# Loading the first six adjacency quarters of a graph-attention kernel as halves

## The reference, cut to what matters

```python
def _L0_gnn_ref(input1, input2, adj, a1, a2):      # N = M = 4096, D = 128
    e = input1 @ a1 + (input2 @ a2).T
    e = jnp.where(e > 0, e, 0.2 * e)
    att = jnp.where(adj > 0, e, NEG)
    att = jax.nn.softmax(att, axis=1)
    deg = jnp.sum(adj, axis=1, keepdims=True)
    att = att * deg
    att = GAMMA * att + (1.0 - GAMMA) * adj
    return att @ input2

x = x + _L0_gnn_ref(_layernorm(x, axis=-1), L0_gnn_input2, adj, L0_gnn_a1, L0_gnn_a2)
x = x + _L0_ffn_ref(_layernorm(x, axis=-1)[None], L0_ffn_weight, L0_ffn_bias)[0]
```

## Time and profile before

| | us |
|---|---|
| median of 3 runs (377.69 to 378.69) | 378.52 |
| the profiled execution: its time | 376.63 |
| the profiled execution: its span | 374.8 |
| PE busy in that span | 357.4 (95%) |
| DVE busy | 311.4 (83%) |
| ACT busy | 252.9 (67%) |
| POOL busy | 146.6 (39%) |
| the 16 DMA engines: POOL's queue, share of their span | 47.0% |

### The profile page before, as it was taken

How to read it: one execution, slowest core, us unless ns; L and a number is a source line. 1 busy time by engine, 2 the same in 40 slices (tenths; PEclk the granted TensorE clock), 3 DMA queues, 4 the chain that set the end, 5 groups by cost and what they waited for, 6 DMA issues and landing times.

```text
span 374.8 us, 8950 instructions
## 1 busy us (share of the span) xinstructions
PE 357.4 (95%) x3199; PEld 313.6 (84%) x3199; DVE 311.4 (83%) x787; ACT 252.9 (67%) x616; POOL 146.6 (39%) x258
## 2 busy tenths in 40 slices
PE   5689999999999799999999999999999999999992
PEld 5578888888888688888888888888888888888881
DVE  5998989969999768879788888989687887999832
ACT  5799896697588568392947749294874929897100
POOL 4594713805262532608043260806225160703111
PEclk9999999999999999999999999999999999999998
DMA  7999959492959596694929487591958830121000
GB/s 251 202 214 202 218 110 183 78 192 45 171 119 174 117 144 136 81 202 89 204 45 181 91 145 139 96 199 42 160 118 117 160 72 2 32 26 44 30 18 30
DMA packets 34646, 45.72 MB, mean 122 GB/s; under 512 B 18084, under 2 KB 25896, under 8 KB 34600
## 3 DMA queue, kind: packets, MB, share of 16 engines
q0 software_dynamic: 9216, 33.56, 47.0%
q1 hardware_dynamic: 25384, 11.56, 16.4%
HBM read 74.84 MB, written 3.82 MB: 210 GB/s over the span
## 4 chain that ended last, share of the span: by engine, by line
PE 77%; DMA 8%; issue 5%; DVE 3%; POOL 2%; ACT 2%; SPq 1%; POOLq 0%; DVEq 0%
PE acc_u L760 23%; PE acc_v L763 23%; PE acc_y L742 21%; PE acc_v L742 4%; DMA adj_all<-adj 4%; PE acc_u L742 3%; DMA late<-block_rows 3%; PE acc_y L731 2%; PE small L725 2%; ACT steep L554 2%; DMA s_rows<-pre_s 1%; DVE plus L972 1%; POOL adj_all L409 1%; SPq L330 1%; PE acc_u L731 0%
## 5 line engine op out<-in xcount | busy, mean ns | idle before, releaser
L554 ACT ACTIVATE steep<-s_bc,steep_s 128x256 bf16<-128x256 f32 x512 | 218.2, 524 | 13.1 <-DMA s_bc<-s_rows 6.6
L763 PE MATMUL acc_v<-weights_v,minus 128*128 128x258 f16 x896 | 198.1, 272 | 0.0
L760 PE MATMUL acc_u<-weights_u,plus 128*128 128x258 f16 x896 | 198.1, 273 | 0.0
L742 PE MATMUL acc_y<-weights_y,adj_all 128*128 128x257 f16 x896 | 101.3, 273 | 0.4 <-DMA adj_all<-adj 0.4
L742 PEld LDWEIGHTS acc_y<-weights_y,adj_all 128*128 128x128 bf16 x896 | 86.8, 97 | 12.5 <-DMA adj_all<-adj 0.7
L760 PEld LDWEIGHTS acc_u<-weights_u,plus 128*128 128x128 bf16 x896 | 86.7, 97 | 12.0
L763 PEld LDWEIGHTS acc_v<-weights_v,minus 128*128 128x128 bf16 x896 | 87.1, 97 | 11.4
L972 DVE TENSOR_TENSOR plus<-adj_all,steep 128x2048 bf16<-128x2048 bf16 x64 | 80.6, 1260 | 18.5 <-ACT steep L554 18.5
L975 DVE TENSOR_TENSOR minus<-adj_all,plus 128x2048 bf16<-128x2048 bf16 x64 | 79.9, 1248 | 2.2
L568 ACT ACTIVATE num<-acc_u,ac 128x129 f32<-128x129 f32 x32 | 11.5, 364 | 87.0 <-PE acc_u L760 85.3
L453 POOL TENSOR_SCALAR post_var<-post_mv 128x2 f32<-128x2 f32 x15 | 3.3, 218 | 163.9 <-issue 133.8
(11 more groups left out here) (130 smaller groups left out, 300.1 us busy)
## 6 DMA issues: line engine op xcount, KB each, us to landing
adj_all<-adj POOLq DMA_DIRECT2D x64, 512.0 KB, 10.9
x_in<-x SPq DMA_DIRECT2D x16, 128.0 KB, 5.1
plus<-in SPq DMA_DIRECT2D x4, 512.0 KB, 5.5
out<-late SPq DMA_DIRECT2D x15, 128.0 KB, 4.6
s_bc<-s_rows SPq DMA_DIRECT2D x13, 128.0 KB, 7.4
block_rows<-late SPq DMA_DIRECT2D x13, 128.0 KB, 1.7
late<-block_rows SPq DMA_DIRECT2D x52, 32.0 KB, 11.8
s_rows<-pre_s SPq DMA_DIRECT2D x13, 1.0 KB
```

What stands on the lines that cost most here:

```text
L554: ins = nc.scalar.activation(steep[:, h, k, :].rearrange("q (t p) -> q t p", t=TILES), s1_tiles[b], ACT.Relu, bias=steep_s2[:, jt:jt + 1], ...
L742: ends[t] = nc.tensor.matmul(acc[t][:, 0:width], left[:, jt, cols(t)], right[:, jt, :, :].rearrange("p a b -> p (a b)")[:, 0:width], start ...
L760: last_u = nc.tensor.matmul(acc_u[t][:, 0:2 * WC], plus[b][:, jt, cols(t)], w_u[:, jt, :, :].rearrange("p a b -> p (a b)"), start=(jt == 0 ...
L763: last_v = nc.tensor.matmul(acc_v[t][:, 0:2 * WC], minus[b][:, jt, cols(t)], w_v[:, jt, :, :].rearrange("p a b -> p (a b)"), start=(jt == ...
```

## The change

Six quarters, (0,0) to (0,3), (1,0) and (1,1), are loaded as two DMAs of 4 column blocks each. The first half raises a new semaphore `half_landed[n, q]`, the second half the old `adj_landed[n][q]`. For these quarters Y's products come from a new `half_pairs`: wait for the half, 8 matmuls, wait for the second half, 8 matmuls. The DVE masks of these quarters wait for both semaphores. On POOL, `centre` is made directly after the identity, ahead of the first load.

```diff
+SPLIT = [(0, 0), (0, 1), (0, 2), (0, 3), (1, 0), (1, 1)]
...
             def load_adj(n, quarters=range(QUARTERS)):
                 for q in quarters:
+                    if (n, q) in SPLIT:
+                        mid = q * QJ + QJ // 2
+                        nc.gpsimd.dma_start(
+                            adj_b[n][:, q * QJ:mid, :].rearrange("p a b -> p (a b)"),
+                            adj[n, q, :, 0:QJ // 2 * CHUNK]).then_inc(half_landed[n, q], 16)
+                        nc.gpsimd.dma_start(
+                            adj_b[n][:, mid:mid + QJ // 2, :].rearrange("p a b -> p (a b)"),
+                            adj[n, q, :, QJ // 2 * CHUNK:QJ * CHUNK]).then_inc(adj_landed[n][q], 16)
+                        continue
...
+            pool.wait_ge(consts_ready, 1)
+            nc.gpsimd.tensor_scalar(centre[:, :], ident[:, :], -1.0 / D, None, ALU.add).then_inc(centre_ready, 1)
             pool.wait_ge(in2_landed[0], 16)
             load_adj(0, (0,))
             row_sums(0, 0)
             load_adj(0, (1, 2, 3))
             load_adj(1)
-            pool.wait_ge(consts_ready, 1)
-            nc.gpsimd.tensor_scalar(centre[:, :], ident[:, :], -1.0 / D, None, ALU.add).then_inc(centre_ready, 1)
             factor_columns()
...
+            def half_pairs(n, q):
+                acc = acc_y if n else first_y
+                ends = [None] * TILES
+                for h in range(2):
+                    pe.wait_ge(adj_landed[n][q] if h else half_landed[n, q], 16)
+                    for k in range(QJ // 2):
+                        for t in range(TILES):
+                            jt = q * QJ + h * QJ // 2 + (k + t * QJ // 4) % (QJ // 2)
+                            ends[t] = nc.tensor.matmul(
+                                acc[t][:, 0:WC + D], adj_b[n][:, jt, cols(t)],
+                                w_y[:, jt, :, :].rearrange("p a b -> p (a b)")[:, 0:WC + D],
+                                start=(q == 0 and h == 0 and k == 0),
+                                stop=(q == QUARTERS - 1 and h == 1 and k == QJ // 2 - 1))
+                return ends
...
-                pe.wait_ge(adj_landed[n][q], 16)
-                ends = pair(acc_y if n else first_y, adj_b[n], w_y, q, WC + D)
+                if (n, q) in SPLIT:
+                    ends = half_pairs(n, q)
+                else:
+                    pe.wait_ge(adj_landed[n][q], 16)
+                    ends = pair(acc_y, adj_b[n], w_y, q, WC + D)
...
             def masks(n, q, b, f):
...
+                if (n, q) in SPLIT:
+                    dve.wait_ge(half_landed[n, q], 16)
```

More of the change, by code:

```diff
@@ L175, in gnn_ffn @@
         adj_landed = [[sem(f"adj_landed{b}_{q}") for q in range(QUARTERS)] for b in range(BUFS)]
+        half_landed = {k: sem(f"half_landed{k[0]}_{k[1]}") for k in SPLIT}
         x_landed = [sem(f"x_landed{b}") for b in range(2)]
```

## The result

| | before | changed |
|---|---|---|
| median of 5 runs, us | 378.52 (377.69 to 379.17) | 381.26 (380.33 to 381.69) |
| ratio to before, 95% interval | 1 | 1.0071 (1.0042 to 1.0100) |
| the profiled execution: its time / its span | 376.63 / 374.8 | 380.33 / 377.9 |
| last instruction of DVE starts at | 368.99 | 371.62 |

The changed kernel is slower, by 2.7 us. The forecast was 378.0 with a range up to 379.4.

A forecast was written before the change was run, and what follows sets the result against it. PE, busy 95% of the span, was taken as the bound, with time to be had only in its waits. A capped gain of 0.83 us less 0.3 us queue cost gave 0.5 us less: 378.0 us, range 377.2 to 379.4.

The forecast's parts named there:

- The gain of the early matmuls: At (1,0), 8 of 16 matmuls done before the second half lands, so U of (0,0) starts 0.88 us earlier.
- The next landing: At (1,3), landing at 31.98 us, PE running earlier meets the whole quarter, capping the gain at 0.83 us.
- The cost of the halves: On POOL's load queue, smaller pieces add 0.05 us per quarter, 0.3 us for six quarters.
- the far bound: Upper limit of the halves' queue cost, from the other queue's 39 ns per packet: 0.35 us per quarter, 2.1 for six.
- the POOL step: One more issue (0.54 us) ahead of the row sums is hidden; twelve loads end at 16.1 us, before factor columns' 17.40.
- The first: Rival: halves load the queue more than 0.14 us per quarter, making the kernel slower, 378.9 to 379.8 us; chance 0.2.
- The second rival: Gain hidden at 126.98 us if the turned rows' DMA ends with other traffic, not its issue: 378.5 us; chance 0.1.
- Both sides move together, and so does the 1.9 us wait: From the start to chunk 2's turned rows at 126.98 us, PE and DVE shift equally, so the gain reaches the end.
- That the first landings don't matter: At the start, PE's gain on (0,0) to (0,3) is lost waiting for the next quarter; only (1,0)'s wait counts.
- crumbs: PE's waits other than 3.5 us for adjacency quarters and 1.9 us for turned rows, taken as small.
- signs of being wrong: (1,0)'s second half landing after 24.8 us, (1,3)'s last load issued after 17.4, or a longer wait at 126.98.

The follow-up runs named there:

- the base without the wait: Kernel before, but PE turns chunk 2's rows instead of memory: 374.46 us, 0.9908; the pair on it: whole change 376.90, halves waited for whole 377.88 us.
- row_halves: Changed kernel with each half as 64 partitions with full 8 KB rows, both halves waited for before the work: 378.46 us, 1.0027 to the kernel before.
- halves_wait_whole: Changed kernel with the same twelve halves, but Y waits for both and runs its 16 matmuls in one piece: 381.70 us, 1.0101 to the kernel before.
- only_1_0: Changed kernel with only quarter (1,0) loaded as halves, the other quarters whole: 377.98 us, 0.9997 to the kernel before.

## Why the prediction was wrong

**The gain of the early matmuls** was of the right size: 0.88 us by the forecast, 1.0 us by the medians of the pair of kernels on the base without the wait (0.6 by the ratios, 1.3 by the last instruction). The next landing was right too: the cap at (1,3), near 32 us, is the wait of 0.39 us at 32.07 when nothing else is disturbed. In the changed kernel it never came to that, since PE was already late at (1,0).

**The cost of the halves is the step that failed.** The forecast took 0.05 us per quarter, 0.3 us in all, from the parts of `input2`, and named 2.1 us as the far bound. It measured 3.4 us (2.9 by the ratios), beyond the bound. Some of this is not packets: `row_halves`, with as many issues, the same POOL stretch and rows of 8 KB, cost 0.8 us over its before. What is left for the packets is 2.6 us by the medians and 1.9 by the ratios (2.8 by either for `halves_wait_whole` less `row_halves`), so at the bound or beyond it. Two things were mis-sized. First, the price by packet: the `input2` rows are packets of 4 KB too, but of a load without a cast, issued by SP on the other queue. Second, the cost was taken as a constant per quarter, and it isn't: 187 ns for a packet in the first 8 to 10 us of a series that starts from a nearly empty queue, 156 to 159 later, which is as fast as whole quarters (305 and 290 ns for twice the data, which is 153 and 145 for half). The slow stretch falls just on the quarters that PE waits for. 0.37 MB missing at 18 us, at 0.2 MB per us, are 1.8 us, and (1,0) was 2.3 us late. By `row_halves`, 0.17 of the 0.37 MB is missing with long rows too.

**POOL.** The forecast added one issue, 0.54 us, to the row sums and called it hidden. The instruction behind two issues took 0.93 us more as well. The stretch to the next load grew by 0.84 us (3.81 against 2.97; `pre_s` became shorter by 0.71), the row-sum product on PE went from 9.20 to 10.73, of which 0.69 is the late `input2`. What should have been priced is not the row sums but the queue: the twelve loads behind them start later while only 1 MB is in flight. The rest of the POOL step held: the issues ended at 17.07 (16.1 forecast), and `d_lifted` followed at 18.05; the columns ended at 25.26, two microseconds before PE came to them.

**The rivals.** The first, a cost of the halves above 0.14 us per quarter, is what happened, with a size of 3.4 / 6 = 0.57 us per quarter in all, or 0.43 without what `row_halves` cost, instead of 0.2 to 0.35. I had given it 0.2 and bounded it by the whole-kernel mean of the other queue, mostly packets under 512 B, which says nothing about the start of a series. The second rival, that the wait at the turned rows answers to other traffic, was seen in the other direction: that load took 1.3 us longer and the wait grew by 1.0. The step "Both sides move together, and so does the 1.9 us wait" failed. Without an edit the wait was 1.9 and 2.3 us, with others 2.0 to 3.2; only the kernels without it show shifts at the start one to one at the end.

**The clock** was not in the forecast at all. With the halves it is low before or on Y of (0,0) in every profile, and with the wait at 127 us sometimes behind that. In the changed kernel's profile the start took no harm from it: PE waited for loads five times more, 2.1 us in all, between that stretch and U of (0,0). On the base without the wait it made no difference to the changed kernel. By the executions of before it goes with 3 us between 0.996 and 0.986, so it widens any range drawn from three runs. How much of the 3.4 us it carries was not measured apart.

**That the first landings don't matter** held: Y of (0,0) began 0.3 us earlier and nothing came of it. The prediction called all other waits of PE crumbs. Two were not (2.1 us for the load of `a_pair`, 1.6 for `pre_s` from POOL), but they lie ahead of Y of (0,0), which waits for its load in any case.

**The signs.** Two of the three signs of being wrong came: (1,0)'s second half landed at 26.3 and not by 24.8, and the wait at the turned rows grew. The third did not: (1,3) was issued at 16.5, not after 17.4.

## What to carry to other kernels

When loads are cut smaller to shorten a wait, look at what stands in the queue at that moment, and price the packets of a nearly empty queue by themselves: with the row length halved the queue ran at three quarters of its rate just where PE waited, and at its full rate once it no longer mattered. Cutting by partitions kept the long rows and most of the rate; cutting only the one piece that the consumer waits for, behind a full queue, cost nothing that could be told, and gained nothing that could be told either. And before working on a wait at the start, see whether a later wait scrambles what it saves: taking out the single wait at 127 us was worth 3.6 us, more than any edit here gained at the start.

## What the runs showed of the hardware

- Loads of 4 KB rows with a cast on POOL's queue ran at 156 to 172 GB/s for the first 8 to 10 us of a series that started from a nearly empty queue and at about 206 GB/s after; behind whole quarters two of them ran at 205 from the first (`only_1_0`). Whole quarters with rows of 8 KB ran at 199 to 213 from 10 to 18 us; halves with rows of 8 KB at 181 (`row_halves`). The Trainium skill ("DMA: Bandwidth & Descriptors", Rules for kernel authors and Anatomy of one DMA) prefers large DMAs for their fixed cost of about 2.0 us each. It had the direction of this change right. The runs show no such fixed part for each, since halves issued 0.54 us apart kept the engines at 206 GB/s from 19 to 26 us, and at a fixed count of loads the rows' length made the difference (`row_halves`).
- A POOL instruction (`pre_rstd`, 128 x 2 elements) took 0.84 us behind one DMA issue and 1.76 to 1.77 us behind two in a row, for halves and whole quarters alike; the one behind it took 0.94 and 0.22 to 0.23 us, which gives most of that back. What the first of the two waits for is not settled.
- TensorE's granted clock fell to its lower level (1.2 GHz) before 18 us in seven profiles of eighteen, and in six right behind a wait of 2.0 to 3.2 us in an otherwise full program; more warming products at the start of the kernel before changed nothing.
- What makes small packets slow when the queue was nearly empty stays open. Not tried: the same halves without the cast, or on SP's queue.
